# Row maxima handed over without a transpose: strided query tiles and one transfer straight from the column tile

## The chip, the cores and the metric

One core of a Trainium2 chip runs the whole kernel. The metric is the device time of one execution in microseconds (us); lower is better. The kernel's engines are TensorE (PE in the profile, with its weight loads as PEld), VectorE (DVE), ScalarE (ACT), GpSimd (POOL) and SyncE (SP), whose queue issues all DMA transfers.

## The reference

```python
x = x + attention(groupnorm(x))          # x: (16, 512, 32, 32) fp32

# groupnorm: 32 groups of 16 channels, no weights
# attention, per batch element, T = 1024 tokens of C = 512 values:
xs = reshape(x, (B, T, C))
q, k, v = (einsum('btc,hcd->bhtd', xs, W) for W in (Wq, Wk, Wv))   # 8 heads of 64
scores = einsum('bhtd,bhsd->bhts', q, k) / sqrt(64)
att = softmax(scores, axis=-1)
out = einsum('bhts,bhsd->bhtd', att, v)
out = concat_heads(out) @ Wproj + bproj
```

## The kernel before

All matrices are fp32 and are split into a high part (rounded to the fp32r format that PE multiplies) and a low part (the rest), so a product takes two or three matmuls. The 16 batch elements with 8 heads each make 128 heads, worked through one after the other; each head is a step of 16 slots (`BLOCKS`). In slot i PE computes the transposed scores of block i + 3 (`scores`, L708 and L709: 128 keys by 512 queries, two halves of queries times eight key tiles) and the product with v of block i (L881 to L883). ScalarE takes the exponential twice (L899), once in full and once rounded; GpSimd (L1294) or VectorE (L1043) subtracts the two for the low part.

**The row maxima.** The softmax subtracts each query's maximum. In the transposed scores a query is a column, so the maximum can't be an activation bias; it is instead an extra row of the contraction: row D = 64 of `q_lm` holds the negated maximum of each of the 1024 queries, and k has a row of ones there. The maxima come from untransposed scores of the next head, 16 row blocks (`row_scores`, L715: 128 queries by 512 keys, one matmul each), two PSUM banks (`SM`) taken in turn. Row block j covers query tile t and key half `half`, from `row_of(j)`: blocks 0 to 7 are the queries 0 to 511, blocks 8 to 15 the others. VectorE reduces each to a column of `smax` (`take_max`, L1106) and after blocks 7 and 15 combines the key halves into four columns of `nmax` (`combine`, L1111), negated. Column t of `nmax` has the queries t * 128 to t * 128 + 127 along the partitions.

**The way to the row.** PE transposes four columns of `nmax` into a bank (`turn_rows`, L700, 4 x 128); VectorE copies that to four partitions of an unused corner of `q_lm` (`take_rows`, L1117); SP waits for the copy (`mt_used`) and moves the four partitions of 512 bytes into row 64 (`max_row`, L546). PE waits for the transfer (`mrow_in`) before the first scores of each half.

**Order.** What PE does beside scores and v product is written out by hand in `WORK`: for each kind of head (plain, values, norm, tokens, next, proj, rows, end) and slot, a list before and a list after the v product. Entries are the projections for later heads (qk, qn, v), transposes of x (xt), group statistics, the output projection, `row` (one row block) and `mt` (one `turn_rows`; the number is the half: 1 for the second half of the queries, which comes early in the head after). A `row` or `mt` takes the next of the two `SM` banks; `turns` notes whose bank it takes over, and `turn_free` waits for that user. VectorE and SP follow the same lists one slot later. SP is one queue in order: besides `max_row` it issues `twice` (L553, L555: the copy of q and k to the other 64 partitions, four transfers per head, after which PE may start that head's row blocks), `den_to_square` (L572) and `inv_to_rows` (L577, L579: the softmax denominators to a 32 x 16 square, back through DRAM to 64 partitions), and the loads and stores of x.

Of the kernel before, what the change touches and what calls it, by code (L numbers as in the profile page):

```python
# [27 lines left out]
        ((("qn", 0, 5),), (("qn", 0, 1), ("mt", 1, 1))),  # L28
# [7 lines left out]
        ((), (("mt", 0, 1),)),  # L36
# [10 lines left out]
        ((), (("v", 1, 1), ("mt", 1, 1))),  # L47
# [5 lines left out]
        ((), (("mt", 0, 1), ("qn", 0, 2))),  # L53
# [11 lines left out]
        ((), (("qn", 0, 1), ("mt", 1, 1))),  # L65
# [6 lines left out]
        ((("row", 0, 2),), (("qn", 0, 1), ("mt", 0, 1))),  # L72
# [12 lines left out]
        ((("xt", 1, 4), ("mt", 1, 1)), (("row", 0, 2), ("xt", 2, 4))),  # L85
# [5 lines left out]
        ((), (("mt", 0, 1), ("mean", 1, 1))),  # L91
# [28 lines left out]
        ((), (("mt", 1, 1),)),  # L120
# [8 lines left out]
        ((), (("proj", 6, 12), ("mt", 0, 1))),  # L129
# [7 lines left out]
        ((), (("mt", 1, 1), ("row", 0, 2))),  # L137
# [7 lines left out]
        ((), (("mt", 0, 1), ("row", 0, 1))),  # L145
# [9 lines left out]
        ((), (("mt", 1, 1),)),  # L155
# [55 lines left out]
def fillers(h, has_next, proj):  # L211

    slots, done = [], {}
    for sides in WORK[step_kind(h, has_next, proj)]:
        slot = []
        for side, items in enumerate(sides):
            for kind, a, n in items:
                if kind in ("row", "mt"):
                    slot += [(side, kind, a, 0, 1)] * n
                    continue  # L220
                if kind == "v" and h in (1, 2):
                    a += 4 + 2 * (h - 1)
                lo = done.get((kind, a), 0)
                done[kind, a] = lo + n
                slot.append((side, kind, a, lo, lo + n))
        slots.append(slot)
    assert all(n == UNITS[kind] for (kind, a), n in done.items())
    return slots
# [9 lines left out]
class Plan:  # L238


    def __init__(self, batches):
        self.prologue = [("mean", 0), ("var", 0), ("mean", 1), ("var", 1)]
        self.prologue += [("qk", 0), ("qk", 1), ("qn", 0), ("qn", 1), ("v", 0), ("v", 1), ("v", 2), ("v", 3)]
        self.place = {("start", 0, e): (n % 2, n // 2) for n, e in enumerate(self.prologue)}
        used = [len(self.prologue) // 2] * 2
        self.steps, self.takes = {}, {}
        for section, ks in (("first", [0]), ("body", range(1, 9)), ("last", range(1, 8))):
            if section == "last":
                used = [body_start[b] + self.per_batch[b] * (batches - 1) for b in range(2)]
            if section == "body":  # L250
                body_start = list(used)
            for k in ks:
                slots = fillers(k % 8, section != "last", k == 8)
                ended, holder, takes = [-2, -1], [None, None], [[] for _ in range(BLOCKS)]
                for s, slot in enumerate(slots):
                    for side, kind, a, lo, hi in slot:
                        if kind in ("row", "mt"):
                            continue
                        if lo == 0:
                            bank = ended.index(min(ended))  # L260
                            assert ended[bank] < s - (side == 0)
                            holder[bank], ended[bank] = (kind, a), BLOCKS
                            self.place[section, k, (kind, a)] = (bank, used[bank])
                            used[bank] += 1
                        if hi == UNITS[kind]:
                            taken = max(s + 1, TAKE_QN if kind == "qn" else 0)
                            ended[holder.index((kind, a))] = taken - 1
                            takes[taken].append((kind, a))
                self.steps[section, k], self.takes[section, k] = slots, takes
            if section == "body":  # L270
                self.per_batch = [used[b] - body_start[b] for b in range(2)]
        for t in range(8):
            self.place["last", 8, ("proj", t)] = (t % 2, used[t % 2] + t // 2)


class Step:


    def __init__(self, eng, it, section, k, plan):
# [14 lines left out]
        self.turns, user = [], [None, None]  # L294
        for kind, a in [(e[1], e[2]) for slot in self.slots or [] for e in slot if e[1] in ("row", "mt")]:
            n = sum(e[0] == "row" for e in self.turns)
            bank = len(self.turns) % 2
            self.turns.append((kind, n if kind == "row" else a, bank, user[bank]))
            user[bank] = (kind, n if kind == "row" else a)
# [19 lines left out]

    def turn(self, kind, a):  # L320

        return next(e for e in self.turns if e[:2] == (kind, a))
# [11 lines left out]
def attention_block(nc, x, Wq, Wk, Wv, Wproj, bproj, out):  # L334
# [15 lines left out]
    with ExitStack() as ctx:  # L350
# [42 lines left out]
        nmax = sb("nmax", [P, TT])  # L393
        mrow = q_lm[96:100, 0, 0:2 * P].rearrange("p (a q) -> p a q", a=2)
# [37 lines left out]
        mt_done = sem("mt_done")  # L432
        mt_used = sem("mt_used")
# [44 lines left out]

        def mt_taken(eng, s, a):

            eng.wait_ge(mt_used, s.heads(2, 0 if a else 1, 2 if a else 1))
# [45 lines left out]
        def _(sp):  # L527
# [16 lines left out]
            def max_row(half, slot):  # L544

                sp.dma_start(q_lm[D:D + 1, slot, half * 512:(half + 1) * 512].bitcast(F32),  # L546
                             mrow[:, half, :].bitcast(F32)).then_inc(mrow_in[half], 16)
# [17 lines left out]
            sp.wait_ge(mt_used, 1)  # L565
            max_row(0, 0)
# [27 lines left out]
            def step(s):  # L594
                first = s.section == "first"
                for i in range(BLOCKS):
                    if i == s.den_slots[1] and not first:
                        den_to_square(s, -1, 1)
                    for a in s.issued(i - 1, "mt"):
                        mt_taken(sp, s, a)  # L600
                        max_row(a, (s.k + 1 - a) % 2)
# [48 lines left out]
        def _(pe):  # L650
# [47 lines left out]
            def turn_rows(a, turn):  # L698

                nc.tensor.transpose(ps[SM + turn][0:4, 0:P], nmax[:, a * 4:(a + 1) * 4], ident[:, :]).then_inc(mt_done, 1)  # L700

# [10 lines left out]
            def row_scores(slot, j, turn):  # L712

                t, half = row_of(j)
                nc.tensor.matmul(ps[SM + turn][:, :], q_hh[:, slot, t * P:(t + 1) * P],  # L715
# [39 lines left out]
            for j in range(BLOCKS):  # L755
                if j == 11:
                    pe.wait_ge(mt_used, 1)
                elif j == 10:
                    pe.wait_ge(rows_used, 10)
                elif j >= 2:  # L760
                    pe.wait_ge(rows_used, j - 1)
                row_scores(0, j, (j + (j > 9)) % 2)
# [6 lines left out]
                if j == 9:  # L769
                    pe.wait_ge(nmax_ready, 1)  # L770
                    pe.wait_ge(rows_used, 9)
                    turn_rows(0, 0)
# [6 lines left out]

            def turn_free(s, user):  # L780

                if user is None:
                    pe.wait_ge(rows_used, s.heads(BLOCKS, 1))
                    pe.wait_ge(mt_used, s.heads(2, 0, 1))
                elif user[0] == "row":
                    pe.wait_ge(rows_used, s.heads(BLOCKS, 1, user[1] + 1))
                else:
                    mt_taken(pe, s, user[1])
# [18 lines left out]
            def other_work(s, i, side):  # L807

                j = s.rows_in(i)[0] if s.rows_in(i) else 0
                for at, kind, a, lo, hi in s.slots[i]:  # L810
                    if kind == "row":
                        if at == side:
# [4 lines left out]
                            _, _, bank, user = s.turn("row", j)  # L817
                            turn_free(s, user)
                            row_scores((s.k + 1) % 2, j, bank)
                        j += 1  # L820
                        continue
                    if at != side:
                        continue
                    if kind == "mt":
                        _, _, bank, user = s.turn("mt", a)
                        turn_free(s, user)
                        pe.wait_ge(nmax_ready, s.heads(2, 0 if a else 1, 2 if a else 1))
                        turn_rows(a, bank)
                        continue
# [208 lines left out]
        def _(dve):  # L1038
# [69 lines left out]
            def combine(half, used):  # L1108

                dve.wait_ge(rows_used, used)  # L1110
                nc.vector.tensor_reduce(nmax[:, 4 * half:4 * half + 4],  # L1111
                                        smax[:, 8 * half:8 * half + 8].rearrange("p (t a) -> p t a", a=2),
                                        AX.X, ALU.max, negate=True).then_inc(nmax_ready, 1)

            def take_rows(half, turn, count):
                dve.wait_ge(mt_done, count)
                nc.vector.tensor_copy(mrow[:, half, :], ps[SM + turn][0:4, 0:P]).then_inc(mt_used, 1)  # L1117
# [41 lines left out]
            for j in range(BLOCKS):  # L1159
                take_max(j, j + 1, (j + (j > 9)) % 2)  # L1160
# [4 lines left out]
                if j == 7:  # L1165
                    combine(0, 8)
                if j == 9:
                    take_rows(0, 0, 1)
                if j == 11:
                    start_take("v", 1)  # L1170
            combine(1, BLOCKS)
# [5 lines left out]
            def step(s):  # L1177
                first = s.section == "first"
                end = s.h == 7 and not s.has_next
                for i in range(BLOCKS):  # L1180
# [10 lines left out]
                    for side, kind, a, lo, hi in s.slots[i - 1] if i else ():  # L1191
                        if kind == "row":
                            take_max(hj, s.heads(BLOCKS, 1, hj + 1), s.turn("row", hj)[2])
                            if hj in (7, 15):
                                combine(hj // 8, s.heads(BLOCKS, 1, hj + 1))
                            hj += 1
                        if kind == "mt":
                            take_rows(a, s.turn("mt", a)[2], s.heads(2, 0 if a else 1, 2 if a else 1))
# [192 lines left out]
```

## Time and profile before

| | us |
|---|---|
| median of 3 runs | 4464.39 |
| lowest and highest run | 4460.46, 4466.83 |
| the profiled execution, its own time | 4464.95 |
| its span, first to last instruction | 4463.1 |
| PE busy in it | 4421.6 |
| ACT busy | 2995.6 |
| POOL busy | 2862.6 |
| DVE busy | 2615.5 |

The profile is of one execution. Busy time counts an engine's instructions as a union; matmuls overlap in it, their ends being modelled, so the distance between the starts of two matmuls says more of PE than the length of one. In the timeline a row is: start us, length us, engine, line, operation, names written and read, shapes, count, and in brackets the idle time before it and who ended it.

### The profile page before, as it was taken

How to read it: one execution, taken by the hardware profiler on the slowest of the kernel's cores; microseconds unless marked ns; L12 is line 12 of the kernel's file. 1: busy time of each engine (PE TensorE's matmuls, PEld its weight loads, DVE VectorE, ACT ScalarE, POOL GpSimd, SP SyncE). 2: the span in 40 equal slices, each digit the busy share in tenths (PEclk: the TensorE clock that was granted, in tenths of full speed). 3: DMA queues.
4: the chain of work that ended last, by engine and by line, in shares of the span. 5: the costliest groups of instructions: out<-in, count | busy, mean ns of one | idle time of the engine just before them, and what ended most of it. 6: DMA issues, size and time to landing. Idle time of an engine off the chain costs nothing.

```text
span 4463.1 us, 61817 instructions
## 1 busy us (share of the span) xinstructions
PE 4421.6 (99%) x20864; PEld 3610.2 (81%) x20864; DVE 2615.5 (59%) x5063; ACT 2995.6 (67%) x5644; POOL 2862.6 (64%) x2227
## 2 busy tenths in 40 slices
PE   8999999999999999999999999999999999999999
PEld 7888888887888888888888888878888888888886
DVE  6665656656565565656656566465664656646554
ACT  5766757667576675766757567575775757757576
POOL 5666656666666566665666656666666666566566
PEclk9999999999999999999999999999999999999999
DMA  2111111111112111111121111211111111121101
GB/s 77 38 53 48 37 59 36 55 46 38 59 34 60 42 37 59 39 59 41 34 60 40 60 39 32 60 40 62 38 33 59 48 59 33 36 65 39 59 25 56
DMA packets 156826, 211.42 MB, mean 47 GB/s; under 512 B 56545, under 2 KB 57569, under 8 KB 156513
## 3 DMA queue, kind: packets, MB, share of 16 engines
q1 hardware_dynamic: 156512, 207.47, 16.3%
q8 instruction: 169, 2.77, 0.3%
q14 instruction: 145, 1.18, 0.1%
HBM read 105.12 MB, written 34.08 MB: 31 GB/s over the span
## 4 chain that ended last, share of the span: by engine, by line
PE 92%; DVE 3%; ACT 2%; POOL 1%; issue 1%; DMA 1%; SPq 0%; DVEq 0%; POOLq 0%; ACTq 0%
PE bank L663 15%; PE bank L715 10%; PE bank L881 10%; PE bank L708 10%; PE bank L709 10%; PE bank L883 10%; PE bank L882 10%; PE bank L675 8%; PE bank L693 8%; DVE xs L1073 1%; PE bank L681 1%; POOL prob_l L1294 1%; DVE smax L1106 1%; ACT prob_h L899 1%; PE bank L700 1%
## 5 line engine op out<-in xcount | busy, mean ns | idle before, releaser
L1294 POOL TENSOR_TENSOR prob_l<-prob,prob_h 128x512 fp32r<-128x512 f32 x1660 | 2142.2, 1294 | 1415.4 <-ACT prob_h L899 1381.5
L1106 DVE TENSOR_REDUCE smax<-bank 128x1 f32<-128x512 f32 x2048 | 1346.5, 684 | 843.9 <-PE bank L715 832.8
L899 ACT ACTIVATE prob<-bank 128x512 f32<-128x512 f32 x2048 | 1231.2, 601 | 675.2 <-PE bank L709 577.4
L899 ACT ACTIVATE prob_h<-bank 128x512 fp32r<-128x512 f32 x2048 | 1230.6, 601 | 394.0 <-PE bank L883 304.5
L708 PE MATMUL bank<-q_hh,k_hl 128*128 128x512 f32 x2048 | 830.0, 405 | 0.0
L881 PE MATMUL bank<-prob_h,vh 128*128 128x512 f32 x2048 | 816.0, 398 | 6.9 <-ACT acc L1018 4.4
L709 PE MATMUL bank<-q_lm,k_h 65*128 65x512 f32 x2048 | 811.6, 396 | 0.0
L882 PE MATMUL bank<-prob_h,vl 128*128 128x512 f32 x2048 | 806.5, 394 | 0.0
L883 PE MATMUL bank<-prob_l,vh 128*128 128x512 f32 x2048 | 806.0, 394 | 0.0
L715 PE MATMUL bank<-k_hl,q_hh 128*128 128x512 f32 x2048 | 709.0, 396 | 4.7 <-DVE smax L1106 4.5
L1043 DVE TENSOR_TENSOR prob_l<-prob,prob_h 128x512 fp32r<-128x512 f32 x388 | 315.6, 813 | 300.1 <-ACT prob_h L899 299.9
L881 PEld LDWEIGHTS bank<-prob_h,vh 128*128 128x128 f32 x2048 | 388.2, 190 | 102.7 <-ACT acc L1018 20.0
L715 PEld LDWEIGHTS bank<-k_hl,q_hh 128*128 128x128 f32 x2048 | 379.0, 188 | 98.3 <-DVE smax L1106 10.4
L1321 POOL TENSOR_TENSOR o<-acc,inv_b 64x512 f32<-64x512 f32 x256 | 354.7, 1386 | 160.5 <-DMA inv_b<-inv_dram 144.0
L883 PEld LDWEIGHTS bank<-prob_l,vh 128*128 128x128 f32 x2048 | 384.7, 188 | 88.3
L708 PEld LDWEIGHTS bank<-q_hh,k_hl 128*128 128x128 f32 x2048 | 385.6, 188 | 86.2 <-issue 6.3
L882 PEld LDWEIGHTS bank<-prob_h,vl 128*128 128x128 f32 x2048 | 387.8, 189 | 80.0
L709 PEld LDWEIGHTS bank<-q_lm,k_h 65*128 65x128 f32 x2048 | 386.1, 189 | 67.2
L663 PE MATMUL bank<-xh,wqk_h 128*128 128x512 f32 x1024 | 405.9, 396 | 4.4 <-DVE xs L1245 2.0
L663 PE MATMUL bank<-xh,wqk_l 128*128 128x512 f32 x1024 | 402.7, 393 | 0.0
L663 PE MATMUL bank<-xl,wqk_h 128*128 128x512 f32 x1024 | 401.3, 392 | 0.0
L675 PE MATMUL bank<-wv_h,xh 128*128 128x256 f32 x1024 | 288.3, 282 | 0.0
(83 smaller groups left out, 5052.6 us busy)
## 6 DMA issues: line engine op xcount, KB each, us to landing
xs<-in_x SPq DMA_DIRECT2D x252, 256.0 KB, 2.9
q_hh<-q_hh SPq DMA_DIRECT2D x256, 128.0 KB, 2.2
k_hl<-k_h SPq DMA_DIRECT2D x256, 128.0 KB, 2.3
inv_b<-inv_dram SPq DMA_DIRECT2D x256, 128.0 KB, 2.8
out_x<-xs SPq DMA_DIRECT2D x128, 256.0 KB, 2.0
q_lm<-q_lm SPq DMA_DIRECT2D x256, 2.0 KB
den<-acc SPq DMA_DIRECT2D x256, 2.0 KB, 1.7
inv_dram<-inv SPq DMA_DIRECT2D x256, 2.0 KB, 1.4
```

The source lines that it names most:

```text
L663: last = nc.tensor.matmul(w[:, :], weight[:, c, head, :], moving[:, c, cols], start=u == 0, stop=u == 3 * CH - 1)
L675: last = nc.tensor.matmul(w[:, j * 256:(j + 1) * 256], weight[:, c, t], moving[:, c, vcols], start=cp == 0, stop=cp == 3 * CH - 1)
L693: last = nc.tensor.matmul(w[:, :], left[:, o_set, c, :], right[:, c, :], start=u == 0, stop=u == 3 * CH - 1)
L708: nc.tensor.matmul(s_bank[:, :], k_hl[:, slot, keys], q_hh[:, slot, queries], start=True, stop=False)
L709: nc.tensor.matmul(s_bank[:, :], k_h1[0:D + 1, slot, keys], q_lm[0:D + 1, slot, queries], start=False, stop=True).then_inc(scores_ready, 1)
L715: nc.tensor.matmul(ps[SM + turn][:, :], q_hh[:, slot, t * P:(t + 1) * P], k_hl[:, slot, half * 512:(half + 1) * 512], start=True, stop=Tru ...
L881: nc.tensor.matmul(ps[bank][:, :], v_hi_op, prob_h[:, ring, :], start=t == 0, stop=False)
L882: nc.tensor.matmul(ps[bank][:, :], v_lo_op, prob_h[:, ring, :], start=False, stop=False)
L883: nc.tensor.matmul(ps[bank][:, :], v_hi_op, prob_l[:, ring, :], start=False, stop=t == TT - 1).then_inc(pv_done, 1)
L899: return nc.scalar.activation(out, ps[ST + bank][:, :], ACT.Exp, scale=SCALE)
L1106: nc.vector.tensor_reduce(smax[:, 2 * t + half:2 * t + half + 1], ps[SM + turn][:, :], AX.X, ALU.max).then_inc(rows_used, 1)
L1294: nc.gpsimd.tensor_tensor(prob_l[:, r3, :], prob[:, ring2, :], prob_h[:, r3, :].bitcast(F32), ALU.subtract).then_inc(prob_l_pool, 1)
```

## The change

Query tile t of the row blocks no longer is 128 neighbouring queries, but every fourth query of its half: queries 512 * (t // 4) + t % 4 + 4p for p = 0 to 127. Column t of `nmax` then holds at partition p a query next to that of column t + 1, so partition p of the four columns is the 16 bytes that belong at queries 4p to 4p + 3 of the half. One transfer takes `nmax[:, 4 * half : 4 * half + 4]`, partition by partition, into row 64 of `q_lm`. The transpose, the copy, the `mt` entries, `turns` and `turn_free` are gone; the two banks simply alternate with the row block. SP issues the transfer in the slot behind the one with row block 7 or 15 and waits for `nmax_ready`. `combine` first waits until the transfer of the head before has read `nmax`.

```diff
-                if kind in ("row", "mt"):
+                if kind == "row":
...
-        nmax = sb("nmax", [P, TT])
-        mrow = q_lm[96:100, 0, 0:2 * P].rearrange("p (a q) -> p a q", a=2)
+        nmax = sb("nmax", [P, TT], F32R)
...
-            def max_row(half, slot):
+            def max_row(half, slot, count):
+                sp.wait_ge(nmax_ready, count)
                 sp.dma_start(q_lm[D:D + 1, slot, half * 512:(half + 1) * 512].bitcast(F32),
-                             mrow[:, half, :].bitcast(F32)).then_inc(mrow_in[half], 16)
+                             nmax[:, 4 * half:4 * half + 4].bitcast(F32)).then_inc(mrow_in[half], 16)
...
-            sp.wait_ge(mt_used, 1)
-            max_row(0, 0)
+            max_row(0, 0, 1)
+            max_row(1, 0, 2)
...
-                    for a in s.issued(i - 1, "mt"):
-                        mt_taken(sp, s, a)
-                        max_row(a, (s.k + 1 - a) % 2)
+                    for hj in s.rows_in(i - 1) if i else ():
+                        if hj in (7, 15):
+                            max_row(hj // 8, (s.k + 1) % 2, s.heads(2, 1, hj // 8 + 1))
...
-            def turn_rows(a, turn):
-                nc.tensor.transpose(ps[SM + turn][0:4, 0:P], nmax[:, a * 4:(a + 1) * 4], ident[:, :]).then_inc(mt_done, 1)
...
                 t, half = row_of(j)
-                nc.tensor.matmul(ps[SM + turn][:, :], q_hh[:, slot, t * P:(t + 1) * P],
+                first = 512 * (t // 4) + t % 4
+                nc.tensor.matmul(ps[SM + turn][:, :], q_hh[:, slot, first:first + 4 * P - 3:4],
                                  k_hl[:, slot, half * 512:(half + 1) * 512], start=True, stop=True).then_inc(rows_ready, 1)
...
-                            _, _, bank, user = s.turn("row", j)
-                            turn_free(s, user)
-                            row_scores((s.k + 1) % 2, j, bank)
+                            pe.wait_ge(rows_used, s.heads(BLOCKS, 1, j - 1))
+                            row_scores((s.k + 1) % 2, j, j % 2)
...
-            def combine(half, used):
+            def combine(half, used, read):
                 dve.wait_ge(rows_used, used)
+                if read:
+                    dve.wait_ge(mrow_in[half], read)
...
-            def take_rows(half, turn, count):
-                dve.wait_ge(mt_done, count)
-                nc.vector.tensor_copy(mrow[:, half, :], ps[SM + turn][0:4, 0:P]).then_inc(mt_used, 1)
```

In `WORK` every `mt` entry is taken out, and nothing else is changed in it.

## Rows read from the trace of the kernel before

**Rows 1.** The page, engines' busy time and shares; PE and granted clock in 40 slices.
```profile
PE 4421.6 (99%) x20864; PEld 3610.2 (81%) x20864; DVE 2615.5 (59%) x5063; ACT 2995.6 (67%) x5644; POOL 2862.6 (64%) x2227
...
PE   8999999999999999999999999999999999999999
...
PEclk9999999999999999999999999999999999999999
```

**Rows 2.** The page, chain of work that ended last, shares by engine.
```profile
PE 92%; DVE 3%; ACT 2%; POOL 1%; issue 1%; DMA 1%; SPq 0%; DVEq 0%; POOLq 0%; ACTq 0%
```

**Rows 3.** Timeline of PE, eight matmuls of 512 columns apart.
```profile
1004.04 0.39 PE L708 MATMUL bank<-q_hh,k_hl 128*128 128x512 f32 x1
...
1005.90 0.40 PE L663 MATMUL bank<-xl,wqk_h 128*128 128x512 f32 x1
```

**Rows 4.** Timeline of PEld, then of PE, in the v work before the first head.
```profile
39.98 0.19 PEld L675 LDWEIGHTS bank<-wv_h,xh 128*128 128x128 f32 x1
40.10 0.19 PEld L715 LDWEIGHTS bank<-k_hl,q_hh 128*128 128x128 f32 x1
...
40.10 0.29 PE L675 MATMUL bank<-wv_h,xh 128*128 128x256 f32 x1
40.22 0.40 PE L715 MATMUL bank<-k_hl,q_hh 128*128 128x512 f32 x1
```

**Rows 5.** Groups by line: count, busy us, mean ns, idle before and who ended it.
```profile
L700 PE MATMUL bank<-ident,nmax 128*4 128x128 f32 x256 | 69.6, 272 | 0.8 <-DVE smax L1106 0.7
...
L700 PEld LDWEIGHTS bank<-ident,nmax 128*4 128x4 f32 x256 | 21.2, 83 | 19.0 <-DVE smax L1106 9.7
...
L1117 DVE CAST q_lm<-bank 4x128 fp32r<-4x128 f32 x256 | 72.6, 283 | 104.0 <-PE bank L700 101.2
```

**Rows 6.** Timelines around a transpose: PE, PEld, and PE at the last one.
```profile
1011.03 0.40 PE L663 MATMUL bank<-xl,wqk_h 128*128 128x512 f32 x1
1011.27 0.27 PE L700 MATMUL bank<-ident,nmax 128*4 128x128 f32 x1
...
1011.64 0.41 PE L709 MATMUL bank<-q_lm,k_h 65*128 65x512 f32 x1
...
1011.27 0.19 PEld L708 LDWEIGHTS bank<-q_hh,k_hl 128*128 128x128 f32 x1 [0.15 <-issue]
...
4412.58 0.40 PE L883 MATMUL bank<-prob_l,vh 128*128 128x512 f32 x1
...
4413.15 0.39 PE L709 MATMUL bank<-q_lm,k_h 65*128 65x512 f32 x1
```

**Rows 7.** Waits: who waited for whom, us in total, times, longest.
```profile
PEld bank L700 <- DVE smax L1106: 9.7, 26, 0.9
```

**Rows 8.** A values head: VectorE's nmax, SP's issues, PE's next row block.
```profile
389.89 0.16 DVE L1111 TENSOR_REDUCE nmax<-smax 128x4 f32<-128x8 f32 x1
...
390.63 0.48 SPq L553 DMA_DIRECT2D q_hh<-q_hh  x1
...
392.44 0.60 SPq L555 DMA_DIRECT2D k_hl<-k_h  x1
...
395.86 0.62 PE L715 MATMUL bank<-k_hl,q_hh 128*128 128x512 f32 x2
...
L546 SPq DMA_DIRECT2D q_lm<-q_lm x256: 599/657/723, 43.8 to 4414.7; - x128
```

**Rows 9.** DMA issues by tile: count, KB each, median us from issue to landing.
```profile
k_hl<-k_h SPq DMA_DIRECT2D x256, 128.0 KB, 2.3
inv_b<-inv_dram SPq DMA_DIRECT2D x256, 128.0 KB, 2.8
...
den<-acc SPq DMA_DIRECT2D x256, 2.0 KB, 1.7
```

**Rows 10.** The last head: nmax written, first scores that need it.
```profile
4398.20 0.16 DVE L1111 TENSOR_REDUCE nmax<-smax 128x4 f32<-128x8 f32 x1
...
4404.64 0.39 PE L708 MATMUL bank<-q_hh,k_hl 128*128 128x512 f32 x1
```

More of the change, by code:

```diff
@@ L27 @@
     "plain": (
-        ((("qn", 0, 5),), (("qn", 0, 1), ("mt", 1, 1))),
+        ((("qn", 0, 5),), (("qn", 0, 1),)),
         ((), (("row", 0, 1),)),
@@ L35 @@
         ((), (("row", 0, 2), ("qn", 1, 1))),
-        ((), (("mt", 0, 1),)),
+        ((), ()),
         ((("qn", 0, 1),), (("row", 0, 1),)),
@@ L46 @@
         ((("v", 0, 17),), (("row", 0, 2), ("v", 1, 7))),
-        ((), (("v", 1, 1), ("mt", 1, 1))),
+        ((), (("v", 1, 1),)),
         ((), (("v", 1, 8), ("row", 0, 2), ("v", 0, 6))),
@@ L52 @@
         ((), (("row", 0, 2), ("qn", 1, 3))),
-        ((), (("mt", 0, 1), ("qn", 0, 2))),
+        ((), (("qn", 0, 2),)),
         ((), (("qn", 1, 2), ("row", 0, 2))),
@@ L64 @@
         ((("qn", 0, 6),), (("row", 0, 2),)),
-        ((), (("qn", 0, 1), ("mt", 1, 1))),
+        ((), (("qn", 0, 1),)),
         ((("row", 0, 2),), (("qn", 0, 1),)),
@@ L71 @@
         ((("row", 0, 1),), (("var", 0, 1),)),
-        ((("row", 0, 2),), (("qn", 0, 1), ("mt", 0, 1))),
+        ((("row", 0, 2),), (("qn", 0, 1),)),
         ((), (("qn", 1, 1), ("qn", 0, 1))),
@@ L84 @@
         ((), (("row", 0, 2),)),
-        ((("xt", 1, 4), ("mt", 1, 1)), (("row", 0, 2), ("xt", 2, 4))),
+        ((("xt", 1, 4),), (("row", 0, 2), ("xt", 2, 4))),
         ((), ()),
@@ L90 @@
         ((("row", 0, 1),), ()),
-        ((), (("mt", 0, 1), ("mean", 1, 1))),
+        ((), (("mean", 1, 1),)),
         ((("row", 0, 1),), (("var", 1, 1),)),
@@ L119 @@
         ((), (("row", 0, 2),)),
-        ((), (("mt", 1, 1),)),
+        ((), ()),
         ((("row", 0, 1),), (("row", 0, 1),)),
@@ L128 @@
         ((), (("proj", 5, 12),)),
-        ((), (("proj", 6, 12), ("mt", 0, 1))),
+        ((), (("proj", 6, 12),)),
         ((), (("proj", 7, 12),)),
@@ L136 @@
         ((), ()),
-        ((), (("mt", 1, 1), ("row", 0, 2))),
+        ((), (("row", 0, 2),)),
         ((), (("row", 0, 1),)),
@@ L144 @@
         ((), (("row", 0, 1),)),
-        ((), (("mt", 0, 1), ("row", 0, 1))),
+        ((), (("row", 0, 1),)),
         ((), (("row", 0, 1),)),
@@ L154 @@
         ((), ()),
-        ((), (("mt", 1, 1),)),
+        ((), ()),
         ((), ()),
@@ L256, in __init__ @@
                     for side, kind, a, lo, hi in slot:
-                        if kind in ("row", "mt"):
+                        if kind == "row":
                             continue
@@ L293, in __init__ @@
         self.out_slots = EARLY_OUT if self.proj else END_OUT if end else OUT_SLOTS
[L294 to L299, printed above, removed]
     def at(self, per_batch, const):
@@ L318, in bank @@
         return bank, n
-    def turn(self, kind, a):
-        return next(e for e in self.turns if e[:2] == (kind, a))
     def issued(self, slot, kind):
@@ L431, in attention_block @@
         v_done = sem("v_done")
-        mt_done = sem("mt_done")
-        mt_used = sem("mt_used")
         proj_done = sem("proj_done")
@@ L477, in entry_taken @@
             eng.wait_ge(taken[bank], before + 1)
-        def mt_taken(eng, s, a):
-            eng.wait_ge(mt_used, s.heads(2, 0 if a else 1, 2 if a else 1))
         def start_taken(eng, kind, a):
@@ L755, in _ @@
             for j in range(BLOCKS):
[L756 to L760, printed above, removed]
+                if j >= 2:
                     pe.wait_ge(rows_used, j - 1)
-                row_scores(0, j, (j + (j > 9)) % 2)
+                row_scores(0, j, j % 2)
                 until = 9 * (j + 1) // 2
@@ L768, in _ @@
                     v_units += hi - lo
[L769 to L772, printed above, removed]
                 if j == 13:
@@ L778, in _ @@
             pe.wait_ge(v_cols, 2)
[L780 to L788, printed above, removed]
             def work_free(s, kind, a):
@@ L822, in other_work @@
                     if at != side:
[L823 to L828, printed above, removed]
                         continue
@@ L1159, in _ @@
             for j in range(BLOCKS):
-                take_max(j, j + 1, (j + (j > 9)) % 2)
+                take_max(j, j + 1, j % 2)
                 if j == 1:
@@ L1165, in _ @@
                 if j == 7:
-                    combine(0, 8)
-                if j == 9:
-                    take_rows(0, 0, 1)
+                    combine(0, 8, 0)
                 if j == 11:
                     start_take("v", 1)
-            combine(1, BLOCKS)
+            combine(1, BLOCKS, 0)
             lo_part(0, 0, lambda: dve.wait_ge(prob_h_ready, 1))
@@ L1192, in step @@
                         if kind == "row":
-                            take_max(hj, s.heads(BLOCKS, 1, hj + 1), s.turn("row", hj)[2])
+                            take_max(hj, s.heads(BLOCKS, 1, hj + 1), hj % 2)
                             if hj in (7, 15):
-                                combine(hj // 8, s.heads(BLOCKS, 1, hj + 1))
+                                combine(hj // 8, s.heads(BLOCKS, 1, hj + 1), s.heads(16, 0, 16))
                             hj += 1
-                        if kind == "mt":
-                            take_rows(a, s.turn("mt", a)[2], s.heads(2, 0 if a else 1, 2 if a else 1))
                     if j not in pool_blocks_of(s, ahead) and not (end and ahead):
```

4 rows, old and new, of the table WORK are left out of this document.

## The prediction

> **What bounds the kernel now.** I read the page from the top: engine shares, slices, chain. TensorE is busy in 4421.6 of 4463.1 us, no other engine in more than 67% of the span, and every slice behind the first has PE and its granted clock at nine tenths or more [rows 1], so it works at the 2.4 GHz level throughout. The chain that ended last is 92% PE [rows 2]. Whatever takes PE's stream a nanosecond less per instruction therefore comes back almost whole; what is saved elsewhere comes back only where PE waits for it.
>
> Next I read the timeline of PE by starts, not by busy times, since matmuls overlap. Eight matmuls of 512 columns without a transpose among them start over 1.86 us, from 1004.04 to 1005.90: a pitch of 0.2325 us [rows 3]. Their weight loads are recorded with 0.19 us each, but that is not what a load occupies: among the 256-column matmuls of the v work, loads of 0.19 us start every 0.12 us, overlapping one another, and so do the matmuls [rows 4]. A load thus occupies at most 0.12 us of the load path, and behind a 512-column matmul 0.2325 - 0.12 = about 0.11 us stand free.
>
> **Removed: 256 transposes on PE.** Their group shows 69.6 us busy, 272 ns each [rows 5], which overstates the price. By starts: from 1011.03 to 1011.64 there are two full pitches (the 512-column matmul and the row matmul behind it) plus the transpose, 0.61 - 0.465 = 0.145 us; at the last of the 256, from 4412.58 to 4413.15, it is 0.57 - 0.465 = 0.105 us [rows 6]. The load row behind the transpose tells why: the weights of L708 could only be loaded from 1011.27 on, when the transpose began, so that load lay bare (idle 0.15, "issue") [rows 6]. I take 0.115 us, nearer the lower end, since most transposes stand like the last one: 256 x 0.115 = 29.4 us. The ends are 256 x 0.105 = 26.9 and 256 x 0.145 = 37.1 us.
>
> Before some transposes PE also waited for a maximum: 9.7 us at the load and 0.8 us at the matmul, 10.5 us in all [rows 5]. A wait of the load costs PE only what exceeds the free 0.11 us; 26 waits [rows 7] cover 2.9 us of the 9.7. Part of the rest would be met by a row matmul waiting for the same bank. I take 4 us, with 0 and 10.5 as ends.
>
> **Removed: 256 copies on VectorE**, 283 ns each, 72.6 us, and 101.2 us in which VectorE stood still for the transposes [rows 5, 7]. VectorE is at 59% and on the chain with 3% [rows 1, 2]; I count nothing for it, with 5 us as the upper end. The combining of smax into nmax stays as it is (0.16 us each [rows 8]).
>
> **Moved: SP's max_row.** It now waits for nmax_ready in the slot behind the one with row 7 or row 15, instead of behind the mt entry. Going through the lists, that is 1 slot earlier at the least (values, half 0: 6 against 7) and at most 7 (proj: 4 against 11); for half 1 it is 3 slots or more. One transfer per half in both versions, so no issue is added. Queued behind it on SP are the twice transfers of q and k, den_to_square and inv_to_rows. In the values heads it now steps ahead of four twice issues: nmax is written from 389.89 to 390.05, the transfer's issue takes 0.66 us (657 ns median), so the first twice issue moves from 390.63 to about 390.7 [rows 8]. Who waits for it is the row matmul at 395.86; even the last of the four, issued at 392.44 and landing 2.3 us later, has over a microsecond to spare [rows 8, 9]. Cost nothing; if that cover were gone, 0.1 us in each of some 30 heads, 3 us.
>
> **Changed: the transfer's shape**, 4 pieces of 512 bytes before, 128 pieces of 16 bytes after. The trace has no such transfer. Nearest is den, one row taken apart into a 32 x 16 square in 64-byte pieces, 1.7 us to landing; inv_b, the longest of the kernel's inner loop, takes 2.8 us [rows 9]. 128 pieces are four times the 32 of the square; even if its 1.7 us grew with the count, the landing would take 6.8 us. The tightest place is the last head: nmax written until 4398.36, first scores matmul that reads it at 4404.64, 6.3 us later [rows 10], and that is the shortest such distance of all 256. So I count nothing, with 1 us as the upper end.
>
> **Added: the wait before the minimum** (mrow_in of the head before). That transfer was issued a whole head, some 35 us, earlier: nothing.
>
> **Changed: the stationary operand of 2048 row matmuls** takes every fourth column of q_hh, 16 bytes apart. No stationary or moving operand of the kernel before is read so; every load in the trace is of neighbouring columns, 188 to 190 ns. From below the price is nothing, since just as many columns are read. From above there is no row. What the rows do give is the cover: 0.11 us behind each 512-column matmul, none behind a 256-column matmul or a transpose. By the order of PE's records 154 of the 2048 row matmuls follow a v matmul (one stands in [rows 4]) and 15 follow an xs transpose. If a load took twice its 0.12 us, the 169 would each lose 0.11 to 0.12 us, some 19 us, and the other 1,879 nothing. I take zero.
>
> The Trainium skill has a rule on this that speaks against the change: SBUF — State Buffer, Specifications (TRN2), says that SBUF wants two hits or more in a 16-byte line for full bandwidth, and that each crossing to a new line pays. The same page (Door 1: The DMA port swizzle) says that four fp32 may be strided free of charge, which is just the stride used here. By the second sentence the sum stands; by the first it would move to B or C below; the page gives no size, and no run here shows it yet.
>
> **Sum.** 4464.95 (the profiled execution; its span is 4463.1) - 29.4 - 4 = 4431.6 us. Its own time is 0.6 us above the median 4464.39, so for the median 4431 us, 0.75% faster. All lower ends: 4464.4 - 37.1 - 10.5 - 5 = 4412; with every extra at nothing: 4464.4 - 26.9 + 1 + 3 = 4442. Under 0.2%, 9 us, I call it no change.
>
> **Rivals.**
>
> A. As summed: 4431 us. Chance 0.62.
>
> B. The strided load takes up to twice as long (0.12 us is itself an upper bound for today's) and is covered behind 512 columns: 4431 + 19 = 4450 us. Chance 0.13. For it speaks that one hit in a line instead of four could halve the rate; against it, nothing in the trace.
>
> C. The other side: the strided load takes more than its cover. The point is where 1,879 loads x the excess over 0.2325 us, plus the 19 us above, eats the 33 us: an excess of 14 / 1879 = 7.6 ns, a load of 0.24 us, twice today's. At three times, 0.36 us, it costs 1,879 x 0.1275 = 240 us and 169 x 0.24 = 41 us: 4431 + 281 = 4712 us. Chance 0.15, spread from 4470 to there. It is one cliff: from free to dear within a tenth of the load.
>
> Beside C stands the first sentence of the Trainium skill's page SBUF — State Buffer quoted above: C is what it would bring if its penalty is more than double.
>
> D. PE's gain turns into waits for ScalarE and GpSimd, whose probabilities PE would then reach sooner. Against it: these engines are at 67% and 64% [rows 1]; PE waits little for them as it is. Two thirds given back: 4465 - 11 = 4454, up to no change. Chance 0.07.
>
> E. The 16-byte pieces take over 6 us to land, and PE stands before the first scores of a head: each microsecond by which a landing is late costs up to 127 us, once per head. Chance 0.03.
>
> **Range.** A's own is 4412 to 4442. With B and most of D: 4415 to 4462, which leaves out C and E (0.18). Faster by over 0.2%: A, most of B and a part of D, 0.73; same: 0.09; slower: C and E, 0.18.
>
> **What the profile after should show.** No group of L700 or L1117; PE's count down from 20864 by 256 [rows 1]; PE starts 0.2325 us apart on both sides of a row matmul; the load group of the row matmul still near 188 ns (A), some 290 ns with PE's pitch intact (B), or over 300 ns and a pitch of more than 0.24 us before each row matmul (C). SP's wait for VectorE's copy becomes one for nmax; PE waits for no q_lm transfer. The step that would make me wrong most dearly is the one without a row: the strided load.

## The result, and the profile after

The changed kernel takes 4471.53 us (median of 20 runs, 4469.10 to 4475.64) against 4465.14 us (20 runs) of the kernel before: ratio 1.0016, 95% interval [1.0009, 1.0022]. It is 0.16% slower where 0.75% faster was forecast; the time lies 40 us above the forecast and outside its range. Two of the seven executions of e4_runs8 (below) took 6139 and 10407 us, and its figures are those of the other five.

The page of the kernel after, engines' busy time, then its chain by engine, then three groups by line and the row of the maxima transfer:

```profile
PE 4419.8 (99%) x20608; PEld 3721.2 (83%) x20608; DVE 2524.0 (56%) x4807; ACT 2989.6 (67%) x5644; POOL 2862.7 (64%) x2227
...
PE 91%; DVE 4%; DMA 1%; ACT 1%; issue 1%; POOL 1%; SPq 0%; DVEq 0%; POOLq 0%; ACTq 0%
...
L696 PE MATMUL bank<-k_hl,q_hh 128*128 128x512 f32 x2048 | 735.7, 409 | 5.5 <-DVE smax L1062 4.0
L696 PEld LDWEIGHTS bank<-k_hl,q_hh 128*128 128x128 f32 x2048 | 589.0, 311 | 69.7 <-DVE smax L1062 5.6
L837 PEld LDWEIGHTS bank<-prob_h,vh 128*128 128x128 f32 x2048 | 390.4, 191 | 93.9 <-ACT acc L974 21.7
...
q_lm<-nmax SPq DMA_DIRECT2D x256, 2.0 KB, 1.9
```

Against [rows 1] the 256 transposes and the 256 copies are gone, and PE is as busy as before. What is new stands in the second group: the weight load of the row matmul (now L696) takes 311 ns instead of 188, while the loads of the scores, the v product and the projections still take 188 to 191 as before. The transfer of 16-byte pieces lands in 1.9 us, much as the square did [rows 9]. DVE has a percent more of the chain than in [rows 2], ACT a percent less.

Where a longer load hurts is seen in the v work ahead of the first head. Timeline of PEld, then of PE, after the change:

```profile
40.19 0.19 PEld L659 LDWEIGHTS bank<-wv_h,xl 128*128 128x128 f32 x1
40.31 0.31 PEld L696 LDWEIGHTS bank<-k_hl,q_hh 128*128 128x128 f32 x1
40.52 0.21 PEld L659 LDWEIGHTS bank<-wv_h,xh 128*128 128x128 f32 x1
...
40.30 0.28 PE L659 MATMUL bank<-wv_h,xl 128*128 128x256 f32 x1
40.42 0.52 PE L696 MATMUL bank<-k_hl,q_hh 128*128 128x512 f32 x1
40.77 0.28 PE L659 MATMUL bank<-wv_h,xh 128*128 128x256 f32 x1
```

The row matmul is recorded as starting at 40.42, 0.12 us behind the 256-column matmul, as in [rows 4]. But its own weights are loaded only at 40.62 (40.31 + 0.31), it is recorded with 0.52 us instead of 0.40, and the matmul behind it comes at 40.77, 0.35 us later, where a 512-column matmul takes 0.2325 us: 0.12 us lost, as much as the load is longer.

A second loss has nothing to do with the load. The table of waits of the kernel after (us in total, times, longest):

```profile
PE bank L669 <- DVE mv L1009: 16.8, 17, 8.0
```

And, from its timeline, PE's group-mean matmul of one tokens head:

```profile
252.90 0.36 PE L669 MATMUL bank<-mv,group_avg 128*128 128x4 f32 x2 [0.79 <-DVE mv L1009]
```

In the kernel before, this matmul waited in the prologue alone, 2 times for 9.8 us; its head started it at 251.05 without a wait. Now it waits once more in each of the 15 batches that prepare a next one. SP's queue and VectorE of the same head, after the change, show whom it waits for:

```profile
243.69 1.06 SPq L608 DMA_DIRECT2D xs<-in_x  x2
247.21 0.52 SPq L530 DMA_DIRECT2D q_lm<-nmax  x1
247.77 0.59 SPq L608 DMA_DIRECT2D xs<-in_x  x1
...
247.02 0.16 DVE L1069 TENSOR_REDUCE nmax<-smax 128x4 fp32r<-128x8 f32 x1
...
251.04 0.69 DVE L1005 BATCH_NORM_STATS2 bn<-xs 128x6 f32<-128x512 f32 x1 [0.88 <-DMA xs<-in_x]
...
252.38 0.37 DVE L1009 BATCH_NORM_AGGREGATE mv<-bn 128x2 f32<-128x6 f32 x4
```

And the same queue in the kernel before:

```profile
243.90 2.08 SPq L624 DMA_DIRECT2D xs<-in_x  x3
248.60 0.56 SPq L572 DMA_DIRECT2D den<-acc  x1
251.97 0.66 SPq L546 DMA_DIRECT2D q_lm<-q_lm  x1
```

Before, the three loads of x went out together, by 245.98, and the maxima transfer six microseconds later. Now SP stands at the maxima transfer until nmax is written, and the last load of x, behind it in the queue, goes out at 247.77. VectorE's statistics wait 0.88 us for it, then PE 0.79 us for the mean.

Matching PE's instructions of the two traces one by one, start to start, gives the sizes: around the transposes 27.7 us less (30.7 without the 15 places where the group mean follows a transpose), beside row matmuls 31.7 us more, before the group mean and the x transposes 6.6 us more. That is 30.7 less and 38.3 more; the spans differ by 6.4 us, so the rest is small.

### The profile page after: what moved, and what is told of

Same layout as the page of the kernel before. It is cut to its first block, busy times and chain, and to the rows that moved or that the text cites. A ratio compares the mean times of both kernels' runs of the same rounds, so it can differ in the third digit from the quotient of the medians.

```text
span 4469.5 us, 60843 instructions
## 1 busy us (share of the span) xinstructions
PE 4419.8 (99%) x20608; PEld 3721.2 (83%) x20608; DVE 2524.0 (56%) x4807; ACT 2989.6 (67%) x5644; POOL 2862.7 (64%) x2227
## 3 DMA queue, kind: packets, MB, share of 16 engines
q1 hardware_dynamic: 191328, 207.48, 16.8%
## 4 chain that ended last, share of the span: by engine, by line
PE 91%; DVE 4%; DMA 1%; ACT 1%; issue 1%; POOL 1%; SPq 0%; DVEq 0%; POOLq 0%; ACTq 0%
PE bank L647 16%; PE bank L696 11%; PE bank L837 10%; PE bank L839 10%; PE bank L688 10%; PE bank L689 10%; PE bank L838 10%; PE bank L659 8%; PE bank L677 8%; DMA xs<-in_x 1%; DVE xs L1029 1%; DVE smax L1062 1%; PE bank L665 1%; DVE prob_l L999 1%; ACT prob_h L855 0%
## 5 line engine op out<-in xcount | busy, mean ns | idle before, releaser
L688 PE MATMUL bank<-q_hh,k_hl 128*128 128x512 f32 x2048 | 817.7, 399 | 0.0
L839 PE MATMUL bank<-prob_l,vh 128*128 128x512 f32 x2048 | 809.5, 395 | 0.0
L696 PE MATMUL bank<-k_hl,q_hh 128*128 128x512 f32 x2048 | 735.7, 409 | 5.5 <-DVE smax L1062 4.0
L696 PEld LDWEIGHTS bank<-k_hl,q_hh 128*128 128x128 f32 x2048 | 589.0, 311 | 69.7 <-DVE smax L1062 5.6
L999 DVE TENSOR_TENSOR prob_l<-prob,prob_h 128x512 fp32r<-128x512 f32 x388 | 296.3, 764 | 324.6 <-ACT prob_h L855 324.4
L839 PEld LDWEIGHTS bank<-prob_l,vh 128*128 128x128 f32 x2048 | 384.9, 188 | 89.0
```

Source lines behind the costliest of these rows:

```text
L688: nc.tensor.matmul(s_bank[:, :], k_hl[:, slot, keys], q_hh[:, slot, queries], start=True, stop=False)
L696: nc.tensor.matmul(ps[SM + turn][:, :], q_hh[:, slot, first:first + 4 * P - 3:4], k_hl[:, slot, half * 512:(half + 1) * 512], start=True, ...
L839: nc.tensor.matmul(ps[bank][:, :], v_hi_op, prob_l[:, ring, :], start=False, stop=t == TT - 1).then_inc(pv_done, 1)
```

## The experiments

Theory 1: the strided load takes away the gain, and SP's new order adds some microseconds. Theory 2, the rival: the new hand-over as such (16-byte pieces, SP's order, bank order, waits) eats it. Where an experiment changes the stride but not the pieces to match (e1, e2, e8, e10), the maxima land at other queries; what it leaves out is the right maximum for each query, and only its time counts.

**Stride undone, and stride alone.** Edit of e1_contiguous to the changed kernel, and of e2_before_strided to the kernel before:

```diff
-                first = 512 * (t // 4) + t % 4
-                nc.tensor.matmul(ps[SM + turn][:, :], q_hh[:, slot, first:first + 4 * P - 3:4],
+                nc.tensor.matmul(ps[SM + turn][:, :], q_hh[:, slot, t * P:(t + 1) * P],
```
```diff
-                nc.tensor.matmul(ps[SM + turn][:, :], q_hh[:, slot, t * P:(t + 1) * P],
+                first = 512 * (t // 4) + t % 4
+                nc.tensor.matmul(ps[SM + turn][:, :], q_hh[:, slot, first:first + 4 * P - 3:4],
```

> The changed kernel with one thing undone: a query tile is again 128 neighbouring queries, so the stationary operand of the row matmuls is read without a stride. The transfer stays as in the change, so the maxima land at other queries of the same half and the softmax is shifted by another query's maximum. Theory 1, the strided load: matching PE's starts one by one between the two traces puts 31.7 us of added distance beside row matmuls; without the stride the row matmul's load goes back from 311 to 188 ns and the time to 4471.5 - 32 = about 4440 us. Theory 2, the new hand-over (transfer of 16-byte pieces, SP's new order, banks taken in plain alternation) eats the gain: the time stays at about 4471 us, at least above 4463.

> The kernel before with one thing added: the row matmuls take every fourth query; transposes, copies and transfers stay, so the maxima land at other queries of the same half. Theory 1: the load takes about 311 ns and the time rises by some 32 us, to about 4497 us. If part of the price comes from what the strided load meets only in the changed kernel, less. Theory 2: within 0.2% of 4465 us.

e1_contiguous took 4441.59 us, ratio to the kernel before 0.9951 [0.9939, 0.9964]; e2_before_strided 4505.39 us, 1.0091 [1.0077, 1.0105]. The load groups of the two:

```profile
L695 PEld LDWEIGHTS bank<-k_hl,q_hh 128*128 128x128 f32 x2048 | 379.0, 188 | 105.0 <-DVE smax L1061 14.0 <-issue 10.4 <-DVE k_hl L1042 1.2
```
```profile
L716 PEld LDWEIGHTS bank<-k_hl,q_hh 128*128 128x128 f32 x2048 | 589.2, 310 | 70.1 <-DVE smax L1107 5.3 <-issue 4.8 <-DVE k_hl L1088 0.8
```

The load goes with the stride and with nothing else, and the time goes with the load: 30 us less without it (4471.5 - 4441.6), 41 us more with it alone. Theory 2 is out as the main cause; that a smaller part of it, SP's order, is real is shown by e5 below. Why the stride costs more in the kernel before than in the changed one is not settled.

**Other strides.** e4_runs8 takes every second query (two transfers per half, 8-byte pieces, issued behind the twice transfers of the slot), e8_stride3 every third.

```diff
-                first = 512 * (t // 4) + t % 4
-                nc.tensor.matmul(ps[SM + turn][:, :], q_hh[:, slot, first:first + 4 * P - 3:4],
+                first = 512 * (t // 4) + 256 * (t % 4 // 2) + t % 2
+                nc.tensor.matmul(ps[SM + turn][:, :], q_hh[:, slot, first:first + 2 * P - 1:2],
...
-                sp.dma_start(q_lm[D:D + 1, slot, half * 512:(half + 1) * 512].bitcast(F32),
-                             nmax[:, 4 * half:4 * half + 4].bitcast(F32)).then_inc(mrow_in[half], 16)
+                for b in range(2):
+                    sp.dma_start(q_lm[D:D + 1, slot, half * 512 + b * 256:half * 512 + (b + 1) * 256].bitcast(F32),
+                                 nmax[:, 4 * half + 2 * b:4 * half + 2 * b + 2].bitcast(F32)).then_inc(mrow_in[half], 16)
...
```
```diff
-                first = 512 * (t // 4) + t % 4
-                nc.tensor.matmul(ps[SM + turn][:, :], q_hh[:, slot, first:first + 4 * P - 3:4],
+                first = 512 * (t // 4) + 43 * (t % 4)
+                nc.tensor.matmul(ps[SM + turn][:, :], q_hh[:, slot, first:first + 3 * P - 2:3],
```

> Between the two: query tiles take every second query, 8 bytes apart, and two transfers per half with 8-byte pieces bring the maxima to the right places. Nothing is left out. If two reads per 16-byte line are enough for full rate, as the Trainium skill's SBUF page says (Specifications (TRN2)), the load stays at 188 ns and the time is about 4440 us. If the load's time grows evenly with the stride (123 ns for three steps more), it is about 229 ns, covered behind 512 columns, and 169 row matmuls lose 0.04 us: about 4447 us. If any stride costs as much as four, 311 ns and 4471 us.

> The changed kernel with query tiles of every third query (12 bytes apart, the four tiles of a half starting 43 queries apart, so some queries are taken twice and some never, and the maxima land elsewhere; the softmax is shifted by other maxima). Only the load's length counts. Loads so far: 188 ns at 4 bytes, 195 at 8, 309 at 16. If the load is bound by the 16-byte lines that it opens, 128 x 16 bytes' worth at stride 4 fits 0.228 us of occupation, 1.78 ns a line, and stride 2 then gives 64 x 1.78 = 114 ns against 107 from the columns, 7 ns more, as measured; stride 3 opens 96 lines, 171 ns, so the load takes 188 - 107 + 171 = 252 ns. If instead only a stride of 16 bytes or more is slow, it stays under 200 ns; if any read with fewer than two hits in its line pays in full, 309 ns.

e4_runs8 took 4452.21 us, ratio 0.9972 [0.9961, 0.9984]; e8_stride3, a single execution, 4455.91 us. Their load groups:

```profile
L697 PEld LDWEIGHTS bank<-k_hl,q_hh 128*128 128x128 f32 x2048 | 392.4, 195 | 93.6 <-DVE smax L1063 10.5 <-DVE k_hl L1044 3.7 <-issue 3.5
```
```profile
L696 PEld LDWEIGHTS bank<-k_hl,q_hh 128*128 128x128 f32 x2048 | 500.0, 253 | 71.1 <-DVE smax L1062 5.4 <-DVE k_hl L1043 3.3 <-issue 2.5
```

Stride 3 came out at 253 ns where 252 had been worked out from the count of 16-byte lines. With stride 2 the load is as good as free, but the time missed the 4440 us: PE waited more, for the group mean (26.3 us in all).

**A third hand-over.** e3_runs4 keeps neighbouring queries and moves each column of nmax by a transfer of its own, four per half, in 4-byte pieces, issued behind the twice transfers of the slot:

```diff
-                sp.dma_start(q_lm[D:D + 1, slot, half * 512:(half + 1) * 512].bitcast(F32),
-                             nmax[:, 4 * half:4 * half + 4].bitcast(F32)).then_inc(mrow_in[half], 16)
+                for t in range(4):
+                    sp.dma_start(q_lm[D:D + 1, slot, half * 512 + t * P:half * 512 + (t + 1) * P].bitcast(F32),
+                                 nmax[:, 4 * half + t:4 * half + t + 1].bitcast(F32)).then_inc(mrow_in[half], 16)
...
```

> A repair: query tiles of neighbouring queries as before the change, no transpose and no copy as in the change, and four transfers per half, each of one column of nmax, 128 pieces of 4 bytes, into 512 bytes of the row. SP issues them behind the twice transfers of the same slot. Nothing is left out. Theory 1: load 188 ns, no transposes, about 4440 us, if the pieces land in the 6.3 us that the tightest head leaves and the 768 further issues of 0.65 us on SP find room. Theory 2: 4471 us or more, since this hand-over is more work than the changed one.

It took 4540.20 us, ratio 1.0169 [1.0155, 1.0183], 100 us off what theory 1 said, though the load was 189 ns and the pieces landed in 2.0 us. Its row of DMA issues, and its waits on PE:

```profile
q_lm<-nmax SPq DMA_DIRECT2D x1024, 0.5 KB, 2.0
```
```profile
PE bank L670 <- DVE mv L1009: 45.2, 17, 8.2
PE bank L696 <- DVE smax L1062: 30.7, 37, 1.9
```

The four issues stand ahead of loads and of other transfers on SP; my condition that the further issues find room there did not hold. The wait for the group mean grows with the number of issues ahead of the x load: 16.8 us with one, 26.3 with two, 45.2 with four.

Two more things stand in this trace. VectorE waited 290 us for `den`, whose issue also stands behind the four, against 128 in e1_contiguous, and its maxima come later: 32 of the 94 us between the traces of the two (4533.6 - 4439.8) lie ahead of row matmuls, 28 before the group mean. And the granted clock falls. PE's timeline, then two stretches with PE's and PEld's busy time first and the granted clock third from the end:

```profile
253.35 0.36 PE L670 MATMUL bank<-mv,group_avg 128*128 128x4 f32 x2 [2.34 <-DVE mv L1009]
254.64 0.63 PE L837 MATMUL bank<-prob_h,vh 128*128 128x512 f32 x1
255.07 0.63 PE L838 MATMUL bank<-prob_h,vl 128*128 128x512 f32 x1
...
240.00:254.00 14.00, 11.66 (x58) 9.28 (x57) 10.12 (x25) 9.78 (x18) 10.92 (x9) 1.00 0.22 66
254.10:257.30 3.20, 3.20 (x10) 2.51 (x10) 1.18 (x4) 1.19 (x2) 0.47 (x1) 0.50 0.04 8
```

Behind a wait of 2.34 us the clock is granted at 0.50, the 1.2 GHz level, and 512-column matmuls start 0.43 us apart instead of 0.2325. Ten of the 15 such waits (2.1 to 2.6 us) are followed by such a stretch, five are not, and one more stretch begins at the end of a 1.9 us wait before a row matmul; in the changed kernel, where PE stands 0.79 us at this place, there is none before the last 30 us. The stretches ahead of the last 60 us of e3_runs4 add up to 41 us, which at half speed lose some 20 us (an estimate). So the waits seem to cost more than their own length, though no run separates the two.

**SP's order alone.** e5_issue_behind_loads is the changed kernel, e7_runs8_behind_loads is e4_runs8, each with one block moved:

```diff
-                    for hj in s.rows_in(i - 1) if i else ():
-                        if hj in (7, 15):
-                            max_row(hj // 8, (s.k + 1) % 2, s.heads(2, 1, hj // 8 + 1))
                     for kind, a in s.takes[i]:
...
                         if kind == "xt" and a < 4:
                             sp.wait_ge(xt_done, s.batches(8, 8 + a + 1))
                             sp.dma_start(xs[:, a, :], xv[s.it + 1, :, 4 + a, :]).then_inc(x_in[a], 16)
+                    for hj in s.rows_in(i - 1) if i else ():
+                        if hj in (7, 15):
+                            max_row(hj // 8, (s.k + 1) % 2, s.heads(2, 1, hj // 8 + 1))
```

> The changed kernel with one move on SP: in each slot the maxima transfer is issued behind the twice transfers and behind the loads of x instead of ahead of them. Nothing is left out. Theory 1 (two causes: the strided load, and SP's wait for nmax that now stands ahead of the last x load of the tokens heads, so that the group statistics come late): SP's move takes back the 6.1 us by which PE waited more for the group mean in the first runs (16.8 us against 10.7) and part of the 3.6 us before the x transposes behind it: 4471.5 - 6 to 9 = 4463 to 4466 us. Rival: the wait is only shifted, since PE's own order makes it late: 4471 us.

> Query tiles of every second query with two transfers of 8-byte pieces, as in e4_runs8, and SP's order of e5_issue_behind_loads. Nothing is left out. In e4_runs8 PE waited 26.3 us for the group mean against 10.7 in the kernel before, since two issues stood ahead of the x load. Theory 1: with the loads ahead of them this goes, 4452.6 - 10 to 16 = 4437 to 4443 us, faster than both kernels. Rival: 4452 us.

e5_issue_behind_loads took 4462.58 us, ratio 0.9992 [0.9983, 1.0001]: 8.9 us less than the changed kernel (8.7 by the spans of the two traces). Its SP queue in the tokens head, by the timeline, and PE's wait, by the waits:

```profile
242.39 4.76 SPq L605 DMA_DIRECT2D xs<-in_x  x3
247.20 0.52 SPq L530 DMA_DIRECT2D q_lm<-nmax  x1
```
```profile
PE bank L669 <- DVE mv L1009: 10.4, 2, 8.0
```

The loads are out ahead of the maxima, and the wait for the mean is back at the prologue's two. e7_runs8_behind_loads took 4434.09 us, ratio 0.9929 [0.9917, 0.9942], with the whole computation in place: 0.7% faster than the kernel before, 37 us faster than the changed one. It is the best full version tried.

**The covered load.** e6_rows_first puts the row entries ahead of the v and xt entries in seven lists, such as:

```diff
-        ((), (("v", 1, 8), ("row", 0, 2), ("v", 0, 6))),
+        ((), (("row", 0, 2), ("v", 1, 8), ("v", 0, 6))),
...
-        ((), (("xt", 0, 4), ("row", 0, 1))),
+        ((), (("row", 0, 1), ("xt", 0, 4))),
```

> The changed kernel with seven slot lists reordered: where a row entry stood directly behind a v or xt entry of the same side, it now stands ahead of it, so that its strided load lies behind a 512-column matmul. Nothing is left out. In the changed kernel's trace the matmul behind such a row matmul starts 349 ns later instead of 235 in the kernel before, 114 ns in each of 170 places; about 155 of them are moved. Theory 1 (the load occupies about 0.23 us and costs only where it isn't covered): 155 x 0.114 = 17.7 us less, about 4454 us. Rival (the strided read slows PE by itself wherever it stands, or the banks' waits do): under 5 us less, about 4468 us.

It took 4454.17 us, ratio 0.9974 [0.9964, 0.9983]: 17.4 us less than the changed kernel, where 17.7 were expected. e9_both joins e5 and e6; e10_contiguous_behind_loads joins e1 and e5.

> The changed kernel with both moves: SP's maxima transfer behind the loads of x (e5_issue_behind_loads, 8.9 us less) and row matmuls ahead of the v and xt work of their slot (e6_rows_first, 17.4 us less). Stride 4 and the single 16-byte-piece transfer stay; nothing is left out. If the two causes are separate, the gains add: 4471.5 - 26.3 = 4445 us. If they share a cause, about 4453 us.

> e1_contiguous (neighbouring queries, maxima landing at other queries of the half) with SP's order of e5_issue_behind_loads. It shows what the hand-over without transposes would give if the stride were free and no load of x late: 4441.6 - 9 = 4433 us, that is 4465 - 32, the sum of the prediction. It also prices stride 2 (e7_runs8_behind_loads, 4434 us): within 2 us, if the 195 ns load is covered. Rival: a further cost of the hand-over stays hidden, and it is above 4438 us.

e9_both took 4445.78 us, 0.9955 [0.9941, 0.9968]: the two gains add. e10_contiguous_behind_loads took 4427.26 us, 0.9917 [0.9903, 0.9930], 6 us under what I expected. Its four executions spread from 4426.96 to 4432.16 us, and the profiled one is the slowest. So differences to it are given by medians and by spans. Stride 2 (e7) is 6.8 us above it by medians, where at most 2 were expected, but only 1.0 us by spans (4430.4 - 4429.4), and e7's row matmuls behind v and xt work lose nothing against it: the rest is within the spread.

## Why the prediction was wrong, by its own steps

**The strided stationary operand is the step that failed.** "I take zero" was said of the only edit without a row, and the load takes 123 ns more. The forecast's picture of cover was right: rival B's place, the row matmuls behind v and xt work, is real: moving some 155 of them gave back 17.4 us (19 forecast for all 169). B let the other 1,879 go free. Stride 4 in full is worth 4462.6 - 4427.3 = 35.3 us (e5 against e10), 31.4 by the spans of the two traces. Matching PE's starts of these two one by one: behind the 170 uncovered row matmuls 19.4 us more, 114 ns each; beside the covered ones 9.1 us more, some 5 ns each; the rest is spread over the stream.

Is that second part the load running over its cover, the cliff of C? The traces speak against it. The interval from the v product's last matmul (L839 in the changed kernel) to a row matmul, a covered place, has a median of 231, 233, 235 and 236 ns at strides 1, 2, 3 and 4 (e10, e7, e8, e5), and the interval behind a row matmul that follows a v matmul 233, 231, 289 and 349. With stride 3 an uncovered load costs 56 ns, so it occupies at most some 0.12 + 0.056 = 0.18 us (an estimate), well inside the cover of 0.23, and yet four of the five nanoseconds are there. What they are stays open. C's sign, a pitch of more than 0.24 us, did not come.

**SP's move was costed at nothing, and cost 8.9 us** with the strided load (e5), and without it 14.3 us by medians, 10.4 by spans (e1 against e10). The step listed what is queued behind max_row (twice, den_to_square, inv_to_rows) and left out the loads of x, which stand in the same slots of the tokens heads. The transfer being issued earlier was taken for harmless; it is SP's wait for nmax that moved ahead of something urgent. The twice transfers, which I did check, made no wait.

**The gain of the hand-over was right.** The sum said 33 us; without the stride and with SP's order mended it is 4465.5 - 4427.3 = 38 us by medians, 4463.1 - 4429.4 = 33.7 by spans. Around the transposes PE's starts are 30.2 us closer in e10 than before, against 29.4 forecast for them and 4 for the waits before them, so about 1 of those 4 came back there. Some 5 us more came where the group mean had stood behind a transpose, which the sum did not have, and as much was lost before the x transposes. From e10 by way of e5 to the changed kernel the steps are 4427.3 + 35.3 + 8.9 = 4471.5 us; as differences along one path they must add up. By way of e1 they are 14.3 for SP's order and 29.9 for the stride.

**The transfer's shape was right**: 16-byte pieces land in 1.9 us median, 3.6 at most; PE never waited for them. The wait before combining cost nothing, as forecast, and nothing in the runs prices VectorE's freed 170 us by itself. The tightest place was misread, though: the distance of 6.3 us is the shortest behind the prologue, and the first head has 4.4 us (nmax written until 42.22, scores at 46.64). Had a landing taken the 6.8 us of the upper estimate, it would have been late there. Likewise not every load was of 188 to 190 ns: those of the x transposes take 140 in both kernels.

Rivals: B's mechanism came true, and SP's order and some nanoseconds at each covered load came on top of it; C's cliff, D and E did not occur. By the prediction's own bound of 0.2% the outcome, 6.4 us or 0.16% slower, is "no change", which had 0.09. The 0.62 for A was too much, since it gave the one unpriced edit as free with no row on its side.

## What to carry to other kernels

A change of access pattern is an edit of its own: ask for the load's length at that stride before anything else, and compare it with the matmul ahead of it, since a load is nearly free only as far as that matmul lasts. When a wait on an in-order DMA queue moves forward, go through every transfer behind it in each kind of step, loads for much later work above all. The pieces of a transfer need not be long: choose the widest piece whose stride the load still takes, here 8 bytes.

## What the runs showed of the hardware

The load of 128 fp32 columns took 188, 195, 253 and 311 ns (means of the load groups of e1, e4, e8 and the changed kernel) at steps of 4, 8, 12 and 16 bytes. From 8 bytes on that is 58 ns for each 4 bytes more, or 1.8 ns for each of the 32 further 16-byte lines that the columns then lie in; between 4 and 8 bytes it is only 7. The 12 bytes were forecast before the run, at 252 ns; the 107 ns for the columns alone in that forecast were measured in no run. Whether the lines count or the span in bytes is open: no step over 16 bytes was run, and up to there both grow alike.

The Trainium skill's page SBUF — State Buffer, Specifications (TRN2), says two hits in a line are needed for full bandwidth; the traces agree, with 7 ns more at two hits in a line and 123 at one. The same page's section Door 1: The DMA port swizzle calls a step of four fp32 free; for this load the measurement says otherwise.

Transfers inside SBUF of 128 pieces landed in 1.9 to 2.0 us at 16 bytes and 2.0 us at 8 and at 4 bytes a piece, so the size of the piece hardly mattered here; the number of issues on SP did, as e3_runs4 and e4_runs8 show.

The granted clock of TensorE fell from 1.00 to 0.50 behind ten of 15 waits of 2.1 to 2.6 us in e3_runs4, and 512-column matmuls then started 0.43 us apart.
